# Layer 0's edges of a four-layer graph network: one load of 16 registers a batch from a 16-bit table, in place of two loads of 8

## The reference

```python
h = jnp.maximum(_layernorm(x), 0.0)
support = jnp.matmul(h, weight)
gathered = support[edge_src] * edge_weight[:, None]
x = x + jax.ops.segment_sum(gathered, edge_dst, num_segments=3125) + bias
```

## Time and profile before

| | us |
|---|---|
| median of 3 runs | 2941.07 |
| lowest and highest | 2940.23, 2944.43 |
| the profiled execution: its span, which is its own time | 3321.3 |
| layer 0's edges in it | 40 to 648 |
| layer 2's edges in it, two stages | 896 to 1513, 1599 to 2250 |

### The profile page before, as it was taken

The page is one execution under the profiler, slowest core; times in us unless marked ns, Lnnn a source line. Parts: engine busy times, 40 slices in busy tenths (PEclk is TensorE's granted clock), DMA queues, the critical chain, the costliest instruction groups (busy, mean ns, idle before and its releaser), DMA issues.

```text
span 3321.3 us, 56445 instructions
## 1 busy us (share of the span) xinstructions
PE 2643.0 (80%) x15058; PEld 1980.1 (60%) x15146; DVE 1663.3 (50%) x6677; ACT 980.3 (30%) x4757; POOL 1410.3 (42%) x1667
## 2 busy tenths in 40 slices
PE   2444545598448888889499998989699999999998
PEld 1444444455337787778367776767566666666665
DVE  4555555597334555554244545444854444444442
ACT  2444555465212333333123333333800000000000
POOL 3666666300156666661445656660232222222210
PEclk9999999999655555555695667677899999999999
DMA  2111111163233333331423333332610000000001
GB/s 77 44 44 45 44 45 44 44 227 114 79 82 91 89 92 92 91 89 46 106 70 83 90 84 90 89 89 59 231 59 18 17 18 18 18 17 18 17 28 42
DMA packets 183897, 227.24 MB, mean 68 GB/s; under 512 B 62447, under 2 KB 146488, under 8 KB 182808
## 3 DMA queue, kind: packets, MB, share of 16 engines
q0 software_dynamic: 50176, 131.74, 14.8%
q1 hardware_dynamic: 122654, 86.45, 8.3%
q10 hardware_dynamic: 10746, 5.37, 0.6%
HBM read 183.92 MB, written 39.48 MB: 67 GB/s over the span
## 4 chain that ended last, share of the span: by engine, by line
PE 62%; DVE 10%; issue 9%; another core or an unknown queue 5%; ACT 3%; ACTq 2%; DMA 2%; SPq 0%; DVEq 0%; POOL 0%; POOLq 0%
PE banks L2510 26%; PE banks L1538 7%; PE banks L1599 4%; PE banks L1596 3%; PE banks L1597 3%; PE banks L1602 2%; PE banks L748 2%; PE banks L1600 2%; DMA arena<-dst_flat 2%; PE banks L537 1%; PE banks L540 1%; DVE arena L524 1%; PE banks L1554 1%; PE banks L2521 1%
## 5 line engine op out<-in xcount | busy, mean ns | idle before, releaser
L2510 PE MATMUL banks<-arena 128*128 128x384 bf16 (+1 forms) x5475 | 879.8, 324 | 0.0
L2510 PEld LDWEIGHTS banks<-arena 128*128 128x128 bf16 x5475 | 535.7, 98 | 341.7
L222 POOL DMA_INDIRECT arena<-value_table,arena x392 | 396.4, 1011 | 487.2 <-DMA ed_table<-arena 267.0
L222 POOL DMA_INDIRECT arena<-gat_table,arena x392 | 389.7, 994 | 347.1 <-PE banks L1602 169.0
L222 POOL DMA_INDIRECT arena<-h_table,arena x392 | 371.8, 948 | 218.0 <-PE banks L540 90.9
L537 PE MATMUL banks<-arena 128*128 128x425 bf16 x392 | 201.8, 515 | 310.2 <-DVE arena L524 179.6
L2493 POOL TENSOR_TENSOR arena<-arena 128x128 f32<-128x128 f32 x225 | 103.3, 459 | 647.5 <-DVE arena L2567 638.2
L2561 DVE TENSOR_REDUCE arena<-banks 128x128 f32<-128x384 f32 x225 | 125.3, 557 | 364.3 <-PE banks L2510 356.7
L1538 PE MATMUL banks<-arena 128*128 128x512 bf16 (+1 forms) x902 | 279.3, 406 | 17.6 <-issue 15.3
L2551 ACT ACTIVATE arena<-arena 128x128 bf16<-128x128 f32 (+1 forms) x200 | 61.9, 309 | 732.4 <-DVE arena L2567 732.4
L1596 PE MATMUL banks<-arena 128*128 128x17 f32 x784 | 227.6, 371 | 43.3 <-issue 27.2
(11 more groups left out here) (282 smaller groups left out, 4601.6 us busy)
## 6 DMA issues: line engine op xcount, KB each, us to landing
adj_rows<-arena SPq DMA_DIRECT2D x1, 20000.0 KB, 54.6
arena<-adj_rows SPq DMA_DIRECT2D x2, 7200.0 KB, 22.0
arena<-h_rows SPq DMA_DIRECT2D x225, 64.0 KB, 1.8
arena<-ed_table SPq DMA_DIRECT2D x784, 0.5 KB
arena<-h_table,arena POOLq DMA_INDIRECT x392
arena<-value_table,arena POOLq DMA_INDIRECT x392
arena<-gat_table,arena POOLq DMA_INDIRECT x392
arena<-adj_rows SPq DMA_DIRECT2D x2, 1600.0 KB, 6.2
```

The source lines that it names most:

```text
L222: return e.indirect_dma_start(into, None, table, bass.IndirectOffsetOnAxis(ap=index.bitcast(U32), axis=0))
L2510: x = e.matmul(acc[:, 0:w], C[:, sb, db * P:(db + 1) * P], old[:, sb, 0:w], start=(sb == 0), stop=(sb == LAST))
```

## The change

A class `Pairs` takes the place of `Windows` in this stage. VectorE writes `FI` and `STEP` as 16-bit integers into a table `FS` of 49 batches, each with eight first nodes and then eight steps; the table is placed at a multiple of four words, ahead of the stage's other tiles. ScalarE reads one batch with one load of 16 registers, where the load of the steps stood. The registers of a batch are freed when the batch after next is loaded, since windows are used one step later than steps.

```diff
+class Pairs:
+    def __init__(self, e, table, tag):
+        self.e, self.table, self.tag, self.regs, self.v = e, table, tag, {}, {}
+
+    def load(self, g):
+        self.free(g - 2)
+        e = self.e
+        regs = [e.alloc_register(f"{self.tag}_{g}_{k}") for k in range(2 * BC)]
+        e.reg_load(regs, self.table[0:1, 2 * BC * g:2 * BC * (g + 1)])
+        self.regs[g] = regs
+        self.v[g] = [e.snap(r, donate=True, min_val=0, max_val=N if k < BC else WIN) for k, r in enumerate(regs)]
+
+    def free(self, g):
+        for r in self.regs.pop(g, []):
+            self.e.free_register(r)
+        self.v.pop(g, None)
+
+    def window(self, ap, c):
+        v = self.v[c // BC][c % BC]
+        if len(ap.shape) == 3:
+            return ap[:, :, bass.ds(v, WIN)]
+        return ap[:, bass.ds(v, WIN)]
+
+    def column(self, ap, c):
+        return ap[:, :, bass.ds(self.v[c // BC][BC + c % BC], 1)]
...
             s2 = Space(at, keep_end)
             s2.get([NP])
+            s2.word += -s2.word % 4
+            FS = s2.get([NC // BC, 2, BC], I16)
...
-                e.tensor_tensor(STEP[:, 0:NC - 1], FI[:, 1:NC], FI[:, 0:NC - 1], ALU.subtract).then_inc(l0_keys, 1)
-                settle()
+                do(e.tensor_tensor(STEP[:, 0:NC - 1], FI[:, 1:NC], FI[:, 0:NC - 1], ALU.subtract))
+                do(e.tensor_copy(FS[:, :, 0, :], FI.rearrange("p (g c) -> p g c", c=BC)))
+                settle()
+                e.tensor_copy(FS[:, :, 1, :], STEP.rearrange("p (g c) -> p g c", c=BC)).then_inc(l0_keys, 1)
                 e.wait_ge(l0_room, 1)
...
-                first, steps = Windows(e, FI, "l0"), Windows(e, STEP, "l0s", WIN)
+                starts = Pairs(e, FS.rearrange("p g k c -> p (g k c)"), "l0")
                 e.wait_ge(l0_keys, 1)
                 for c in range(NC + 2):
                     if 1 <= c <= NC:
                         j = c - 1
-                        if j % 8 == 0:
-                            steps.load(j)
+                        if j % BC == 0:
+                            starts.load(j // BC)
                         e.wait_ge(l0_summed, j + 1)
                         if j >= 4:
                             e.wait_ge(l0_shared, j - 3)
-                        e.activation(SH[:, j % 4, :].unsqueeze(2), steps.column(windows_in(j), j), ACT.Copy).then_inc(l0_kept, 1)
+                        e.activation(SH[:, j % 4, :].unsqueeze(2), starts.column(windows_in(j), j), ACT.Copy).then_inc(l0_kept, 1)
                     if c >= 2:
                         j = c - 2
-                        if j % 8 == 0:
-                            first.load(j)
...
-                        e.activation(first.of(C, j), windows_in(j)[:, 1:, 0:WIN], ACT.Copy).then_inc(l0_counted, 1)
+                        e.activation(starts.window(C, j), windows_in(j)[:, 1:, 0:WIN], ACT.Copy).then_inc(l0_counted, 1)
...
-                        e.activation(first.of(ACC0, j), windows_in(j)[:, 0, 0:WIN], ACT.Copy).then_inc(l0_acc, 1)
+                        e.activation(starts.window(ACC0, j), windows_in(j)[:, 0, 0:WIN], ACT.Copy).then_inc(l0_acc, 1)
...
```

More of the change, by code:

```diff
@@ L560, in act @@
                             e.wait_ge(l0_counted, j)
-                        e.activation(first.of(C, j), windows_in(j)[:, 1:, 0:WIN], ACT.Copy).then_inc(l0_counted, 1)
+                        e.activation(starts.window(C, j), windows_in(j)[:, 1:, 0:WIN], ACT.Copy).then_inc(l0_counted, 1)
                         if j:
                             e.wait_ge(l0_acc, j)
-                        e.activation(first.of(ACC0, j), windows_in(j)[:, 0, 0:WIN], ACT.Copy).then_inc(l0_acc, 1)
-                first.free()
-                steps.free()
+                        e.activation(starts.window(ACC0, j), windows_in(j)[:, 0, 0:WIN], ACT.Copy).then_inc(l0_acc, 1)
+                starts.free(NC // BC - 2)
+                starts.free(NC // BC - 1)
             return Stage(act=act, pool=pool, dve=dve, pe=pe)
```

## The result

The changed kernel takes 2958.0 us against 2946.5 for the kernel before (20 runs of each): a ratio of 1.0041 (95% interval 1.0025 to 1.0057), some 12 us slower (7 to 17 by the interval). A second set of runs of the same two kernels gave 1.0043 (1.0025 to 1.0062). My forecast was 2928, and faster. The measured time lies inside the range of 2866 to 2960, but only by the part that was put there for a rival; the direction was wrong.

The account below looks back on a forecast made before the run. Exposed ScalarE register loads were taken to hold layer 0's edges above the gathers' pace. Profiled: 3321.3 - 77.4 + 0.5 = 3244.4 us; outside, 0.34 of 40 us, 13.7 less 0.5: 2941.1 - 13.2 = 2928 us, range 2866 to 2960.

Parts of the forecast that it names:

- Price of the new load: ScalarE's load of 16 registers per batch in layer 0's edges would take 0.55 us, in place of 1.762 for steps.
- My upper end: Upper estimate for the new 16-register load: 3.5 us, at the steps' price per register.
- The fixed price: ScalarE register loads cost the same whatever the count: 0.54 us for eight registers, 0.80 for one.
- the flag's 0.80: A ScalarE load of a single register, recorded at 801 ns, cited to show the number of registers is not what costs.
- Stalls left without the profiler: Layer 0's edges keep some 40 us of stalls without the profiler, 0.8 us a batch; called the weakest term.
- The first rival: Gathers already set layer 0's pace without the profiler, all 99.8 us are the profiler's: 2941, no change; chance 0.20.
- My objection to it: Against the first rival: layer 2's stages run at a granted clock of 0.50 and 0.72 and may keep other waits.
- Loop under the gathers: In the first rival, a layer 0 batch without 0.70 us steps takes 7.4 + 2.3 = 9.7 us, under the gathers' 10.0.
- The third rival: ScalarE's new load costs by register, 0.22 us each, 3.5 us: slower by 23 us (2964) to 68 us (3009); chance 0.14.
- Its turning point: The third rival decides from a load of about 2.1 us on, where the stall exceeds today's 2.27.
- The fourth: Rival: the load isn't issued a batch ahead but directly before first use, latency exposed; already in the sum, no own chance.
- The copies: Two VectorE copies of 392 elements ahead of the keys' signal, once: 0 to 0.9 us, taken as 0.5.

Follow-up runs that it names:

- e2: Kernel before with the step table moved two words to a multiple of 16 bytes; 1.0000 of the kernel before.
- e1: Changed kernel with its table in 32-bit entries, one load of 16 registers at the same place; 1.0005 of the kernel before.
- e3: Changed kernel's 16-bit table read in two loads of 8 registers at the places of the kernel before; 0.9991 of the kernel before.
- the probe: Kernel before with 14 register loads of varied count, width and alignment ahead of ScalarE's layer 0 loop, registers used; one register takes 0.28 us.
- n2_after: Changed kernel with layer 0's gathers taken away behind the first 16; its loop alone takes 10.13 us for eight chunks.
- n1: Kernel before with layer 0's gathers taken away behind the first 16; its loop alone takes 8.60 us for eight chunks.
- n3: Kernel before with steps at a multiple of 16 bytes and the same gathers taken away; its loop alone takes 7.65 us for eight chunks.
- e5: Changed kernel with its load issued ahead, at chunk 8g + 4 for batch g + 1; 1.0035 of the kernel before.
- e6: Kernel before with the changed kernel's table made by VectorE but not read; 0.9998 of the kernel before.
- b_again: Kernel before, unchanged, profiled once more where it takes 2946 us; 2947.5 us.
- e4: Kernel before with 14 register loads ahead of ScalarE's layer 0 loop, registers unread; the profile has no rows for them, no time given.
- e7: Kernel before with the load of the steps issued twice, the second unread; 98 loads in its profile, 1.0014 of the kernel before.

## Why the prediction was wrong, point by point

- **Price of the new load.** This is the step that failed first, and the one that turned a gain into a loss: 0.55 us in my sum, 3.37 measured. I took 0.55 us as "nearest to the table of first nodes", since the two old tables seemed to differ only by 8 bytes of alignment. That part was right: e2 takes the steps from 1.76 to 0.55. But the new entries differ in width as well, and no row showed a 16-bit load. By e1, e3 and the probe they pay 0.21 us each. My upper end, 3.5 us, was near the true one. The rule of the Trainium skill (Runtime: NRT & Kernel Launch, Instruction fetch mechanics) that I set beside it, some 200 ns a register, was written of loads from HBM; here it fits every load from SBUF but those of aligned 32-bit words in fours, and its estimate of 3.2 us for 16 stands beside 3.37.
- **The fixed price.** I read 0.54 us for eight and 0.80 for one as a price that the number does not change. The probe's load of one register takes 0.28 us, so the flag's 0.80 held something besides. The floor of about 600 ns in the Trainium skill (DMA: Bandwidth & Descriptors, Latency and other measured facts) is not there for these loads: 0.28 and 0.32 us lie below it.
- **Stalls left without the profiler.** I gave the stage 40 us of them, the middle between 20 and all. In the usual execution it has none: its columns go at 10.03 us a batch, its gathers at 10.04. The profiler wasn't the reason; the execution was. With this term at nothing no shorter load can gain anything, as e1 and e2 show. The reading of the earlier trace rows beside it doesn't add up either: some eight steps a batch at 0.65 us too long each would be 5.2 us, and not 2.3. The first rival (gathers already set the pace, no change) had this right. My objection to it, layer 2's clock of 0.50, was none: there the clock is 0.50 in the new profile too, and the gathers at 783.2 to 1298.3 us keep 1.32 us.
- **Loop under the gathers.** 7.4 + 2.3 = 9.7 us in the first rival; measured 8.60. The 7.4 holds: in n2_after four columns away from a load take 3.69 us (302.43 to 306.12), 0.92 each. So the two loads together cost the period 1.2 us and not 2.27. I had read their price off a single gap, 1.90 and 0.37; the chunks right behind a stall follow faster (0.75 us from 310.67 to 311.42 in n2_after), as TensorE's work for them is done, and give part of it back. n1 and n3 show 0.95 for the 1.2 us difference of the steps' load.
- **The third rival** came true in kind: cost by register, load of 3.4 us, slower. It put the loss at 23 to 68 us; measured 12. The 23 is a slip: by the share that I used for the gain, 1.39 of 4.6 us of a remaining 40, it is 12, 2953 us. That this meets the measured loss is luck, since the 40 us were not there. Its turning point, a load of 2.1 us, was too low: the cover of 1.4 us a batch (10.04 - 8.60) lets one load grow from 1.76 to about 3.2 before the loop is slower than the gathers, and 3.1 by the changed kernel's 10.32; both are estimates.
- **The fourth** was right on the code. It is e5 that adds why it doesn't matter: a batch ahead costs the same.
- **The copies**, 0 to 0.9 us, are 1.0 and are covered (e6). Of the changed kernel's 2.6 us at the start, the longer first load is 1.6.

The range reached 2 us past the measured time, which is no merit of the sum: of the mechanism in it only the count of loads, 49, and the covered copies came true.

## What to carry to other kernels

Before costing a saving on one engine, find the pace that holds the stage and the period that each of the others would have alone; a saving under the cover is worth nothing, while a stall that passes it costs at once. If the profiled execution and the runs differ by a tenth, have another profile before pricing anything: half of the stalls may belong to that one execution. When a table is packed to make a load smaller, look at how the load reads it: here half the bytes made a load of sixteen 3.3 times as long (3.37 us against 1.02).

## What the runs showed of the hardware

- On ScalarE's queue a register load from SBUF takes 0.28 us for one register and 0.21 for each more, except that four 32-bit words from a multiple of 16 bytes come together, at about 0.24 us per further four: 0.32, 0.55 and 1.02 us for 4, 8 and 16. 16-bit entries from such a multiple don't: 3.37 us for 16. On SP's queue the eight first nodes take 0.69 us (median of 98 loads in b_again) in place of ScalarE's 0.55.
- The queue stands still for the whole load, needed or not (e5: 3.07 us idle, four chunks ahead of the first use; 1.0035 of the kernel before, no better than the changed one).
- A load whose registers nothing reads is not in the program (e4 and e7): a suspected cost must be doubled with its result in use.
- VectorE's one-hot builds are longer beside GpSimd's gathers: 345, 312 and 267 ns against 330, 288 and 245.
- One chip of those met took 3293 us for the kernel that takes 2946 on the others, with 0.70 us steps in the two queues that load registers. In the chains that ended last of its two profiles, and of the first one, only these two queues show them. What causes them the traces do not show.
